# A fourth Strassen product of 96 matmuls split into seven leaf products of 84

## What is computed

```python
x = x + einsum('bct,bcd->bdt', x, w0[cond])        # 64x64 mixing of rows, by batch
x = x + einsum('bct,bcd->bdt', x, w1[cond])        # the same with w1
base = einsum('bsi,oi->bso', x, W)                 # W: 1024 x 1024, shared by all batches
low = einsum('bsi,bir->bsr', x, lora_A[index])     # rank 32, matrix by batch
x = x + base + 0.5 * einsum('bsr,or->bso', low, lora_B)
x = x + einsum('bsi,boi->bso', x, weight[adapter])  # 1024 x 1024, one of 8 by batch
```

## Time and profile before

| | |
|---|---|
| median of three runs | 383.08 us (382.88 to 383.19) |
| profiled execution, first to last instruction (its span) | 381.9 us |
| TensorE matmuls, busy | 98%, 1738 matmuls |
| VectorE busy | 70% |
| ScalarE busy | 59% |
| GpSimd busy | 30% |

### The profile page before, as it was taken

The page is one execution under the profiler, slowest core; times in us unless marked ns, Lnnn a source line. Parts: engine busy times, 40 slices in busy tenths (PEclk is TensorE's granted clock), DMA queues, the critical chain, the costliest instruction groups (busy, mean ns, idle before and its releaser), DMA issues.

```text
span 381.9 us, 7677 instructions
## 1 busy us (share of the span) xinstructions
PE 375.4 (98%) x1738; PEld 311.7 (82%) x1739; DVE 267.3 (70%) x302; ACT 224.6 (59%) x299; POOL 114.9 (30%) x156
## 2 busy tenths in 40 slices
PE   8999999999999999999999999999999999999995
PEld 5788888888888888888888888888888888888884
DVE  2796978856849888538869367854599635999653
ACT  3589568496246476235465465853677536779443
POOL 0000140100000000024765347563167532676600
PEclk9999999999999999999999999999999999999999
DMA  7985904640368484415437316652256622565223
GB/s 259 399 303 186 366 0 165 218 162 9 111 228 281 151 312 140 165 45 203 144 99 251 86 23 192 206 168 58 57 173 218 167 58 58 200 203 155 60 64 85
DMA packets 24187, 61.38 MB, mean 161 GB/s; under 512 B 1906, under 2 KB 2098, under 8 KB 24114
## 3 DMA queue, kind: packets, MB, share of 16 engines
q1 hardware_dynamic: 23648, 60.10, 47.6%
q10 hardware_dynamic: 466, 0.44, 0.4%
HBM read 52.15 MB, written 8.39 MB: 159 GB/s over the span
## 4 chain that ended last, share of the span: by engine, by line
PE 96%; DMA 2%; SPq 1%; DVE 0%; issue 0%; ACT 0%
PE ps L1526 45%; PE ps L1382 12%; PE ps L1383 12%; PE ps L1384 12%; PE ps L1409 4%; PE ps L1552 4%; PE ps L1618 2%; PE ps L1421 2%; DMA ring_f<-wt 2%; PE ps L1448 2%; PE ps L1567 0%; PE ps L1458 0%; SPq L315 0%; PE ps L1651 0%; DVE ring L906 0%; SPq L321 0%
## 5 line engine op out<-in xcount | busy, mean ns | idle before, releaser
L1526 PE MATMUL ps<-ring,aT 128*128 x752 | 173.2, 389 | 0.0
L1526 PEld LDWEIGHTS ps<-ring,aT 128*128 128x128 f32 x752 | 141.1, 188 | 29.6 <-issue 0.3
L1382 PE MATMUL ps<-ring 128*128 128x512 f32 x208 | 81.1, 390 | 0.0
L1383 PE MATMUL ps<-ring 128*128 128x512 f32 x208 | 81.0, 389 | 0.0
L1384 PE MATMUL ps<-ring 128*128 128x512 f32 x208 | 80.9, 389 | 0.0
L481 POOL TENSOR_TENSOR aT<-xT,aT 128x512 fp32r<-128x512 f32 (+1 forms) x36 | 56.2, 1581 | 47.4 <-ACT aT L766 42.4
L1273 DVE TENSOR_TENSOR ring<-raw,ring 128x1024 f32 (+1 forms) x40 | 61.7, 1600 | 6.2 <-ACT ring L752 6.2
L772 ACT ACTIVATE aT<-ps 64x1024 fp32r<-64x1024 f32 x32 | 32.7, 1023 | 47.5 <-PE ps L1526 47.1
L1301 DVE TENSOR_TENSOR stage<-ps,stage 64x1024 f32<-64x1024 f32 x30 | 36.7, 1222 | 28.9 <-ACT stage L781 28.2
L1290 DVE TENSOR_TENSOR aT<-ps,aT 64x1024 fp32r<-64x1024 f32 x32 | 39.1, 1222 | 21.5 <-ACT aT L772 20.8
L1382 PEld LDWEIGHTS ps<-ring 128*128 128x128 f32 x208 | 39.1, 188 | 8.1
(11 more groups left out here) (98 smaller groups left out, 326.9 us busy)
## 6 DMA issues: line engine op xcount, KB each, us to landing
raw<-w3t SPq DMA_DIRECT2D x40, 512.0 KB, 4.4
ring_f<-xt SPq DMA_DIRECT2D x8, 1024.0 KB, 8.7
raw<-xt SPq DMA_DIRECT2D x8, 1024.0 KB, 5.3
out<-stage SPq DMA_DIRECT2D x30, 256.0 KB, 3.2
ring_f<-wt SPq DMA_DIRECT2D x4, 1024.0 KB, 8.1
xT<-xt SPq DMA_DIRECT2D x3, 1024.0 KB, 10.4
xT<-wt SPq DMA_DIRECT2D x2, 1024.0 KB, 15.9
ring_f<-wt SPq DMA_DIRECT2D x4, 256.0 KB, 5.4
```

Of the source, the lines that this page charges most:

```text
L1382: pe.matmul(dst, hi_of(qw)[:, k, cs], hi_of(qx)[:, k, :], start=start and k == 0, stop=False, skip_group_check=True)
L1383: pe.matmul(dst, hi_of(qw)[:, k, cs], lo_of(qx)[:, k, :], start=False, stop=False, skip_group_check=True)
L1526: last = pe.matmul(acc(i)[:, n, :], x3_split(i, k, start, P), ring[:, bass.ds(off + (part * D + n * 512), 512)], start=(k == 0 and j == 0) ...
```

## The change

The fourth product is taken out of the loop over j. Both row groups are now taken together: A22 (512 by 512) is cut into quarters of 256 by 256, T4 of both j into four blocks of 256 inputs by 512 rows, and Strassen's method is used a second time with seven leaf products of 2 by 2 tiles by 3 matmuls, that is 12 each and 84 in all. Each high and low part is now made for a quarter or for one of the sums of quarters. The low-rank additions stay eight. In TensorE's queue P6 and P7 of j = 1 now come directly behind those of j = 0, and the seven leaves behind both. In TensorE's new queue 12 instructions are gone, the 12 matmuls.

The diff, cut to its core:

```diff
+    LEAF = (("L1", "A11", "B11"), ("L5", "S1", "T1"), ("L2", "A12", "B21"), ("L6", "S2", "T2"), ("L3", "S4", "B22"),
+            ("L7", "S3", "T3"), ("L4", "A22", "T4"))
...
+            sp.wait_ge(s("leaf_b"), 3)
             load_kw(w_block(2, 2))
...
-            load_w(4, 2, 2)
-            load_x(6, 2, 0)
+            wait_l2(sp, ("C11", 1, 3))
+            sp.dma_start(a22, w_block(2, 2)).then_inc(s("a22"), 16)
+            sp.wait_ge(s("seed"), HALF)
+            sp.dma_start(t4_of(0), x_block(2, 0)).then_inc(s("B21_0"), 16)
...
+            sp.wait_ge(s("w_lo"), HALF * 4)
+            load_later(1, 1)
             sp.wait_ge(s("T4"), 1)
             load_stg(1, 3)
-            sp.wait_ge(s("T3"), 2)
-            load_stg(1, 1)
-            load_x(9, 2, 1)
+            sp.wait_ge(s("T2"), 2)
+            load_later(2, 1)
+            sp.wait_ge(s("x_lo"), HALF * 7)
             sp.wait_ge(s("T4"), 2)
             load_stg(1, 0)
-            load_w(5, 1, 1)
-            load_x(10, 1, 2)
-            load_x(11, 1, 2)
+            load_w(4, 1, 1)
+            wait_l2(sp, w_last[3])
+            sp.dma_start(x8_raw, x_block(1, 2)).then_inc(s("x_in8"), 16)
+            load_x(9, 1, 2)
             sp.wait_ge(s("T1"), 1)
             load_stg(2, 2)
...
@@ ScalarE @@
+            def leaf_w_sum_hi(name):
+                act.wait_ge(s("leaf_w"), in_leaf_w(name))
+                leaf_w_hi(name)
...
+            def leaf_x_hi(name, before, sum_of=None):
+                wait_l2(act, before)
+                if sum_of is None:
+                    act.wait_ge(s("T4"), 2 if name == "B22" else 1)
+                else:
+                    act.wait_ge(s("leaf_x"), in_leaf_x(sum_of))
+                act.activation(leaf_x[name][0], leaf_x_raw[name], ACT.Copy).then_inc(s("leaf_x_hi"), 1)
...
-            u2(0)
-            x_from(6, None, "T4", 1)
-            w_from(4, None, "A22", HALF)
+            act.wait_ge(s("A22"), HALF)
+            wait_l2(act, ("low", 1, 3))
+            for name in ("A22", "A12", "A11"):
+                leaf_w_hi(name)
+            u2(0, first_two)
+            leaf_w_sum_hi("S1")
+            leaf_w_sum_hi("S3")
+            leaf_w_sum_hi("S2")
+            u2(0, last_two)
+            x_from(6, stg, "T2", 2)
+            leaf_w_sum_hi("S4")
             u3(0, first_two)
-            for pair in range(8, 12):
-                select(pair)
             seed(1, first_two)
-            u3(0, last_two)
-            x_from(7, stg, "T2", 2)
...
+            x_from(7, keep, "T3", 2)
+            u3(0, (2,))
             seed(1, last_two)
...
+            u3(0, (3,))
+            leaf_x_hi("B11", x_last[5])
+            act.wait_ge(s("x_lo"), HALF * 8)
+            u2(1, (0,))
+            leaf_x_hi("T1", x_last[5], "T1")
+            u2(1, (1, 2, 3))
+            leaf_x_hi("B21", x_last[6])
+            leaf_x_hi("T3", x_last[6], "T3")
+            act.wait_ge(s("T4"), 2)
+            u3(1, first_two)
+            w_from(4, None, "S1", 2)
+            u3(1, last_two)
+            leaf_x_hi("B22", x_last[7])
+            leaf_seed()
+            leaf_x_hi("T2", x_last[7], "T2")
+            act.wait_ge(s("leaf_x"), in_leaf_x("T4"))
+            leaf_out("L5", ps_z, out_block(2, 1)[:, 2:4, :], "R22")
+            leaf_x_hi("T4", w_last[3], "T4")
+            x_from(8, x8_raw, "T1", 1)
+            leaf_out("L6", ps_y, out_block(2, 1)[:, 0:2, :], "U2")
...
@@ VectorE @@
+            def leaf_w_first():
+                leaf_w_lo("A22")
+                dve.wait_ge(s("leaf_w"), in_leaf_w("lo A22"))
+                leaf_w_sum("S1", quarter(2, 1), quarter(2, 2), ALU.add)
+                leaf_w_lo("S1")
+                leaf_w_sum("S3", quarter(1, 1), quarter(2, 1), ALU.subtract)
+                dve.wait_ge(s("leaf_w"), in_leaf_w("lo S1"))
+                leaf_w_sum("S2", quarter(2, 2), quarter(1, 1), ALU.subtract)
+            def leaf_w_rest():
+                leaf_w_lo("A12")
+                dve.wait_ge(s("leaf_w"), in_leaf_w("lo A12"))
+                leaf_w_sum("S4", quarter(1, 2), quarter(2, 2), ALU.subtract)
+                for name in ("A11", "S3", "S2", "S4"):
+                    dve.wait_ge(s("leaf_w"), in_leaf_w("S4"))
+                    leaf_w_lo(name)
...
             t4(0)
-            x_los(6)
-            w_los(4, raw_of(w_slot(4)))
+            leaf_w_first()
             t3(1)
             t2(1)
-            x_los(7, stg)
-            x_los(8, keep)
+            x_los(6, stg)
+            leaf_w_rest()
+            x_los(7, keep)
             take(6)
             t4(1)
+            leaf_x_lo("B11")
+            leaf_x_sum("T1", block4(1, 2), block4(1, 1), ALU.subtract, "lo B11")
+            leaf_x_lo("T1")
+            leaf_x_sum("T3", block4(2, 2), block4(1, 2), ALU.subtract, "T1")
+            take()
+            leaf_x_lo("B21")
+            leaf_x_lo("T3")
+            s1()
+            w_los(4, raw_of(w_slot(4)))
+            leaf_x_lo("B22")
+            leaf_x_sum("T2", block4(2, 2), block4(1, 1), ALU.subtract, "lo B22")
+            leaf_x_lo("T2")
+            leaf_x_sum("T4", block4(2, 1), block4(2, 2), ALU.subtract, "T2")
+            leaf_x_lo("T4")
+            t1(0)
+            x_los(8, x8_raw)
+            leaf_add("L2", ps_x, v11, r11, "R11", ("u3", 1))
+            leaf_add(None, tiles2(r22), v22, r22, "V22", ("R22", 1))
+            leaf_add(None, tiles2(r12), v12, r12, "V12", ("U2", 1))
+            leaf_add("L3", ps_z, r12, r12, "R12", ("V12", 1))
+            leaf_add("L7", ps_y, r22, r22, "U3", ("V22", 1))
+            x_los(10, stg)
+            leaf_add("L4", ps_y, v21, r21, "R21")
             x_los(9)
...
@@ TensorE @@
-                product(2, 4 + 3 * j, 1, j, False, True, "seed")
-                product(3, 5 + 3 * j, 1, j, False, True, "u2")
-                for o in range(HALF):
-                    pe.wait_ge(s("u3"), HALF * j + o + 1)
-                    main(4, 6 + 3 * j, ps_l2(1, j, o), o, False, False)
-                    delta2(j, 1, o)
+                product(2, 4 + 2 * j, 1, j, False, True, "seed")
+                product(3, 5 + 2 * j, 1, j, False, True, "u2")
+            leaf(0, ps_x, True, lambda o: bank_free(LEAF_AT + o))
+            leaf(1, ps_z, True, lambda o: bank_free(LEAF_AT + 4 + o), (b_split, 2 * P, 1))
+            leaf(2, ps_x, False, lambda o: (s("leaf_seed"), o + 1), (b_split, 0, 0))
+            leaf(3, ps_y, False, lambda o: (s("leaf_seed"), o + 1))
+            leaf(4, ps_z, False, lambda o: (s("R22"), o + 1), (leaf_b, 0, 1))
+            leaf(5, ps_y, False, lambda o: (s("U2"), o + 1))
+            leaf(6, ps_y, False, lambda o: (s("U3"), o + 1), (b_split, 2 * P, 0))
```

251 lines of the change are left out of this document (172 added, 79 removed).

## The result

| | before | changed |
|---|---|---|
| median of the runs, us | 383.13 (382.88 to 383.66, 4 runs) | 407.27 (405.90 to 407.63, 4 runs) |
| profiled execution: time, span, us | 383.08, 381.9 | 407.63, 405.8 |
| matmuls on TensorE | 1738 | 1726 |
| ratio of the times | | 1.0619, 95% interval 1.0597 to 1.0641 |

The kernel is 6.2% slower: +24.1 us by the medians, +23.9 by the spans. The forecast was 404.5, with a range of 400.5 to 407.5.

What follows compares the result with a forecast made beforehand. The prediction took TensorE, busy 98% of the span, as the bound: number of matmuls times their pace. Stalls of 24.1 us less 2.7 for removed matmuls gave +21.4, so 383.08 became 404.5 us, range 400.5 to 407.5.

Steps and rivals of the forecast that it cites:

- seven named places: Forecast TensorE stalls: P7 of j 0, P6 and P7 of j 1, L5, L7, L4, low-rank pass of P5; together 24.1 us.
- The removed matmuls: 12 matmuls fewer on TensorE, each worth its start-to-start 0.2267 us: 2.7 us less.
- Step 1: P7 of j 0: the third copy `u2` is ready only at 79.4, wanted at 77.1; stall 2.3 us.
- Step 2: P6 of j 1, moved forward by a product: its seed is ready at 91.3, TensorE at 84.8; stall 6.4 us.
- Step 3: P7 of j 1: `u2(1, 1)` comes behind `take(6)`, ready at 109.9, wanted at 104.9; stall 5.0 us.
- Step 4: The leaves: stalls of 2.5 us before L5, 3.5 before L7, 3.8 before L4, some 0.6 at P5's low-rank pass.
- rival (a): TensorE's clock falls to 1.2 GHz after the stalls: 404.5 to 412.5 us, typically 407; chance 0.12.
- last sign of being wrong: The clock's row shows less than 9 between 90 and 155 us and P5 starts later than 151.
- rival (b): Stalls in the leaves are smaller: 394 us if there are none, 396 to 401 in between; chance 0.11.
- (c): Faster: each copy reaches its bank in time and the 12 matmuls are a clean gain, 380.4 us; chance 0.02.
- the bounds of the single terms: Uncertainty of the `leaf_b` shift, a load, some 40 hand-overs and TensorE's restarts: together 402.5 to 406.5 us.

Runs made afterwards that it cites:

- run 1: Kernel before, with 12 of the 96 matmuls of the A22 product left out: 381.33 us.
- run 3: Changed kernel with idle matmuls ahead of L7 (13) and L4 (14) alone: 412.17 us.
- run 9: Changed kernel with plan steps take(6) and take() moved behind the low parts of the last x unit on VectorE: 408.09 us.
- run 6: Changed kernel with ScalarE's last two copies of P6 moved ahead of the high parts of S1, S3 and S2: 407.35 us.
- run 2: Changed kernel with 86 idle matmuls in TensorE's queue ahead of the six waits: 407.29 us.
- run 4: Changed kernel with 14 idle matmuls before L4 alone: 405.94 us.
- run 7: Changed kernel with VectorE's queue alone in another order, same instructions: 396.39 us.
- run 8: Changed kernel with VectorE's and ScalarE's queues both in another order, same instructions: 393.43 us.
- run 10: Changed kernel in its own order, VectorE's added leaf work shrunk to 16 columns of each row piece, all instructions kept: 402.80 us.
- run 12: Kernel of run 8 with 17 idle matmuls before P6 of j 1 and 15 before the low-rank pass of P5: 390.90 us.
- run 11: Kernel of run 8 with VectorE's added leaf work shrunk as in run 10: 395.23 us.
- run 5: Changed kernel with ScalarE's queue alone in another order, some 40 entries moved: 405.07 us.

## Why the prediction was right, and where it was off

**The sign and the mechanism** were right. Pauses came at six of the seven named places, with the named releasers; only the last one, 0.6 us before the low-rank pass, did not.

**The removed matmuls.** Forecast -2.7; run 1 has -2.7 in the stretch concerned, -2.5 in the span and -2.2 in the medians.

**Step 1**, P7 of j 0: forecast 2.3, measured 2.29.

**Step 2**, P6 of j 1: forecast to begin at 91.3 after a wait of 6.4; it began at 91.17 after 4.3. The wait was shorter because P7 ran at half pace and ended 2.0 us later than forecast, at 86.85. In runs 3 and 9, where P7 happened to stay at full pace, the wait was 6.0 and P6 began no earlier.

**Step 3**, P7 of j 1: forecast to resume at 109.9 after 5.0; it resumed at 109.77 after 2.1. Again the half pace of P6 filled the difference.

**Step 4**, the leaves: L5 0.6 (forecast 2.5, again because TensorE came 1.7 later, at 122.5), L7 3.1 (3.5), L4 3.5 (3.8), the low-rank pass nothing (0.6). L4 began at 145.20, forecast 145.7.

**The step that failed** is the sum's silence on the clock. The forecast left TensorE at full pace behind every pause and gave rival (a) a chance of 0.12. The clock did fall, to 0.50, behind the pauses of 2.3, 4.3, 2.1 and 3.5 us. As that rival said, the slow stretches after the first three ate into the next wait and cost nothing (run 6 shows that even a whole wait there is worth nothing). Up to P5 the pauses are 15.9 us in place of 23.5, and 10.2 us (23.4 + 2.7 - 15.9) went into slower matmuls and restarts, where the forecast had none; since VectorE's and ScalarE's queues set where each pause ends, P5 is off by the last stretch alone. It began at 151.28, not at 148.9. With that the prediction's own last sign of being wrong came true, a clock row below 9 between 90 and 155 us and P5 later than 151: the time lies in the forecast's range, and the course of TensorE is that of rival (a), whose "typically 407" is the measured time.

Not all of the 2.4 us at P5 reached the end, though. At full clock (run 2) P5 begins at 148.88, waits 0.7 for x9, and the adapters begin 1.5 us earlier; run 4 has 1.4, and 1.3 in the median. So of the 2.8 us by which 407.27 exceeds 404.5 the clock accounts for some 1.5 at most. Another 0.5 is that even at full clock the adapters begin at 204.67, where 182.73 + 21.4 makes 204.1, and 0.4 is that the part from there on took 199.58 us in the changed kernel's trace, before 199.17. The rest is within what the runs of one kernel differ by. The Trainium skill ("TensorE: Matmul & The Clock Gate", section on the 56 ns gap) gives 426.7 ns from start to start at 512 columns at the lower clock; L4's 12 steps from 145.76 to 150.88 are 0.4267 each, so here it agrees to the last digit, where its figure at full clock, 215.7, is 5% below this kernel's 226.7.

**Where the reasoning was off though the number was right.** The sum followed the queues in their order, but against rival (b) I argued from amounts: 22 us of work for 18 us of room. Runs 7, 8 and 10 say otherwise. Taking away nearly all of that work in the changed order gives back 4.5 us; giving the queues a better order with all of the work gives back 13.8 with ScalarE's part and 10.9 without. Two parts of the loss are neither. P6 of j 1 is moved forward by a whole product, while its operand still begins with a load that is asked for at 74.4, when T4 is done, lands at 79.4 and then needs two sums, a high part and two low parts: in run 8 all of it is done back to back and P6 still waits 4.1 us. And x9's and x10's loads are asked for once L3 has ended, in run 8 at 125.3, and TensorE wants both units split at 137.6, 12 us later. In the kernel before, the product C21 stood behind both P7s and gave these chains their time; the change took it away there. That these two distances account for the whole of the last 7.8 us was not tried: a different assignment of the buffers would be needed.

**Range and chances.** 407.27 lies in the range for 8 in 10, near its upper end, and above the 402.5 to 406.5 that the bounds of the single terms gave. Rival (a), with a chance of 0.12, did happen in its mechanism; rivals (b) and (c) did not.

## What to carry to other kernels

When TensorE is the bound and never waits, price a cut in matmuls at their start-to-start time (here 2.5 us for 12), and then follow every queue in its new order, instruction by instruction: that sum gave the change, two reorderings of VectorE's queue and a useless early copy each within 3 us, and was 2 to 5 us too low for the plan steps put off. Ask of each operand not only how much work precedes it but how long its chain of load, sum, high and low part is, since a product moved forward leaves that chain behind. And where pauses of 2 us or more will appear, put the half pace behind them into the forecast as a range, for the last pause at least. Matmuls that compute nothing can hold the clock through it, but have to be tried: of four such kernels one won 2.5 us, one at most 1.3, one nothing, and one lost 4.9.

## What the hardware showed that I had not expected

- Idle matmuls into an unread bank made a kernel 2.5 us faster (run 12). Six pauses' worth of them, 86, cost nothing and gained nothing (run 2), and two pauses' worth made a kernel 4.9 us slower (run 3).
- The granted clock fell behind pauses as short as 2.1 us, but not behind that of 0.6. The same pause does not always bring it: behind the 2.2 to 2.3 us in P7 of j 0 the clock fell in the changed kernel and in run 4, and stayed at 1.00 in runs 3, 7 and 9. Behind L7's pause of 3.1 us there was no half pace in the windows from 138 to 144 us, though shorter pauses had it; and two pauses of 4.04 and 4.05 us were followed by different lengths of half pace (run 11). I can't say from these runs which pause is paid.
- Less work on VectorE made a kernel slower by 1.8 us (runs 8 and 11), through a longer half pace and two loads that followed it.
- The second of two 1 MB loads issued 0.4 us apart landed after 7.3 to 9.3 us, the first after 4.9 to 5.3.
- A pause of 3.1 us in the adapter layer for which the profile names no releaser stood in the trace of run 3 and in no other. Its cause is open. A pause that the profile puts down to "issue" can still have a plain cause in another engine's timeline, as the 3.6 us of run 5 has.
